# A four-layer graph network on one core: tables between merges and node stages as 4 KB lines by partition

## The reference

```
L0: h = normalised(h W^T + b) * gate;   agg = softmax-weighted sum of h[src] over dst; then a bounded size
L1: agg = sum of weight * (h W_nbr)[src] over dst;  + h W_own + bias
L2: z = leaky((h W_s^T)[src] + (h W_t^T)[dst]);  softmax over src;  sum of h[src] * share over dst, times W_fc^T
L3: messages of 64 features from h[src], four heads, softmax over dst;  sum over dst
```

## Time and profile before

| what | time |
|---|---|
| median of 3 runs | 8230.51 us (8223.3 to 8243.03) |
| profiled execution | 8246.78 us, its span 8245.1 us |
| busy, of the span | PE 71%, PEld 44%, DVE 63%, ACT 38%, POOL 59% |
| DMA | 1450.33 MB, mean 176 GB/s |
| queues (packets, MB, share of 16 engines) | q1: 236788, 752.87, 26.6%; q10: 413792, 410.91, 15.6%; q0: 150656, 285.54, 12.3% |

### The profile page before, as it was taken

How to read it: one execution, slowest core, us unless ns; L and a number is a source line. 1 busy time by engine, 2 the same in 40 slices (tenths; PEclk the granted TensorE clock), 3 DMA queues, 4 the chain that set the end, 5 groups by cost and what they waited for, 6 DMA issues and landing times. The chain is left out here.

```text
span 8245.1 us, 149719 instructions
## 1 busy us (share of the span) xinstructions
PE 5872.9 (71%) x21822; PEld 3639.1 (44%) x21823; DVE 5193.8 (63%) x17420; ACT 3106.2 (38%) x9803; POOL 4876.8 (59%) x6036
## 2 busy tenths in 40 slices
PE   4997999046769998676999877677666769600476
PEld 3771344025544444454444344444324558500365
DVE  5999888034569996455666555555773549633764
ACT  2990355004555553355444311111112557400156
POOL 1557777757622223764777677777567743477442
PEclk8995899568999999898999988888897989855799
DMA  2661000027966665697888755555105987522267
GB/s 90 211 209 19 1 1 1 1 84 238 306 227 246 245 246 192 203 301 258 314 313 311 278 187 188 188 192 184 41 12 177 294 276 226 163 54 55 62 214 228
DMA packets 801333, 1450.33 MB, mean 176 GB/s; under 512 B 136831, under 2 KB 543383, under 8 KB 801236
## 3 DMA queue, kind: packets, MB, share of 16 engines
q1 hardware_dynamic: 236788, 752.87, 26.6%
q10 hardware_dynamic: 413792, 410.91, 15.6%
q0 software_dynamic: 150656, 285.54, 12.3%
HBM read 803.24 MB, written 645.70 MB: 176 GB/s over the span
## 5 line engine op out<-in xcount | busy, mean ns | idle before, releaser
L1176 PE MATMUL merge_banks<-merge_rows,merge_mask 128*128 x6264 | 1648.1, 420 | 686.8 <-SPq L1145 406.1
L1176 PEld LDWEIGHTS merge_banks<-merge_rows,merge_mask 128*128 128x128 f32 x6264 | 1264.8, 209 | 1070.1 <-issue 885.9
L1158 DVE TENSOR_SCALAR merge_mask<-ramp,dst_at,soft_at_step 128x128 f32<-128x128 f32 x2349 | 843.2, 366 | 987.7 <-PE merge_banks L1176 862.0
L1270 POOL DMA_INDIRECT merge_rows<-h,merge_take_i x1176 | 1127.5, 959 | 565.5 <-issue 291.9
L1812 PE MATMUL node_p_out<-w,node_h_t 128*128 128x259 f32 (+2 forms) x4704 | 1439.2, 429 | 26.9 <-ACT node_h_t L1851 25.6
L1208 ACT COPY merge_total<-merge_banks 128x256 f32<-128x256 f32 x1568 | 577.4, 369 | 1164.3 <-PE merge_banks L1176 1053.8
L1725 POOL TENSOR_TENSOR node_inv_std<-node_var,node_minus_half 128x4 f32<-128x4 f32 x392 | 445.8, 1137 | 872.5 <-DVE node_var L1662 537.5
L1812 PEld LDWEIGHTS node_p_out<-w,node_h_t 128*128 128x128 f32 x4704 | 746.7, 191 | 286.7 <-issue 217.4
L1790 PE MATMUL node_p_turn<-ident,node_xn 128*128 128x128 f32 x3136 | 619.7, 280 | 187.4 <-DVE node_xn L1619 100.2
L1812 PE MATMUL node_p_out<-w,node_kept_t 128*128 128x512 f32 x1568 | 741.4, 596 | 0.0
L1790 PEld LDWEIGHTS node_p_turn<-ident,node_xn 128*128 128x128 f32 x3136 | 407.7, 142 | 725.0 <-issue 449.3
(11 more groups left out here) (485 smaller groups left out, 10602.6 us busy)
## 6 DMA issues: line engine op xcount, KB each, us to landing
merge_held<-own ACTq DMA_DIRECT2D x196, 512.0 KB
x<-merge_total ACTq DMA_DIRECT2D x196, 512.0 KB
node_x<-x SPq DMA_DIRECT2D x196, 512.0 KB, 6.2
node_x<-in_x SPq DMA_DIRECT2D x194, 512.0 KB
h<-node_rows_h SPq DMA_DIRECT2D x98, 512.0 KB
merge_held<-h ACTq DMA_DIRECT2D x98, 512.0 KB
mix<-merge_total ACTq DMA_DIRECT2D x98, 512.0 KB
node_mixed<-mix SPq DMA_DIRECT2D x98, 512.0 KB, 4.2
```

The lines of the kernel that those rows point to most:

```text
L1158: ins = nc.vector.tensor_scalar(mask[j][:], k.ramp[:, 0:P], columns(k.dst_at, s), columns(weight, s), ALU.is_equal, ALU.mult)
L1176: nc.tensor.matmul(banks[:, bass.ds(nc.s_assert_within(at[2 * j + 1], 0, (BANKS - 1) * 512, skip_runtime_bounds_check_because=small), D)], ...
L1270: nc.gpsimd.indirect_dma_start(rows[:, (j + n) * D:(j + n + 1) * D], None, table, bass.IndirectOffsetOnAxis(take_i[:, j + n:j + n + 1], 0) ...
```

## The change

The tables that go from a merge to a node stage or from a node stage to a merge's base (mix0, own1, x2, own2, x3) get the turned shape: one line of 4 KB for each partition of a group, tiles as runs of 128 nodes. Node stages 1 to 3 therefore also take their nodes as tiles of 128 neighbours. So in_x of stage 1 is loaded by `tile_rows` (with one more DMA for the last 80 rows, and 16 more to wait for), and the tables that are gathered by node (h1, from_src, to_dst, h2, h3) are stored by `tile_rows`: pieces of 1 KB, of 544 B for h3. Node stage 0, the table h0, merge 0's base and the output of merge 3 stay as they are. Not a byte more is moved, and no compute instruction is added or removed.

```
 merge, hold(q):
-                act.dma_start(held[q.h][:], tile_rows(base, q.H * ROWS)).then_inc(held_got[q.h], 16)
+                if base.shape[1] == G * D:
+                    act.dma_start(held[q.h][:].rearrange("p g f -> p (g f)"), turned_group(base, q.H)).then_inc(held_got[q.h], 16)
+                else:
+                    act.dma_start(held[q.h][:], tile_rows(base, q.H * ROWS)).then_inc(held_got[q.h], 16)
 merge, flush(q):
-                if whole:
+                if out.shape[1] == G * D:
+                    act.dma_start(turned_group(out, q.H), total[q.h][:].rearrange("p g f -> p (g f)")).then_inc(put[q.h], 16)
+                elif whole:
                     act.dma_start(tile_rows(out, q.H * ROWS, whole), total[q.h][:, 0:whole, :]).then_inc(put[q.h], 16)
 node_pass, load(q):
-                sp.dma_start(mixed[q.h][:], group_rows(mixed_in, q.H * ROWS)).then_inc(mixed_got[q.h], 16)
+                sp.dma_start(mixed[q.h][:].rearrange("p g f -> p (g f)"), turned_group(mixed_in, q.H)).then_inc(mixed_got[q.h], 16)
 node_pass, load_x(q):
-                sp.dma_start(x[q.h][0:rows // G], group_rows(x_in, base, rows)).then_inc(x_got[q.h], 16)
+                if layer >= 2:
+                    sp.dma_start(x[q.h][:].rearrange("p g f -> p (g f)"), turned_group(x_in, q.H)).then_inc(x_got[q.h], 16)
+                elif layer == 1:
+                    whole, part = rows // P, rows % P
+                    sp.dma_start(x[q.h][:, 0:whole, :], tile_rows(x_in, base, whole)).then_inc(x_got[q.h], 16)
+                    if part:
+                        begin = base + whole * P
+                        sp.dma_start(x[q.h][0:part, whole, :], x_in[begin:begin + part, :]).then_inc(x_got[q.h], 16)
+                else:
+                    sp.dma_start(x[q.h][0:rows // G], group_rows(x_in, base, rows)).then_inc(x_got[q.h], 16)
 node_pass, store_tables(q):
-                    sp.dma_start(group_rows(table, q.H * ROWS), part).then_inc(t_put[q.h], 16)
+                    if table.shape[1] == G * D:
+                        sp.dma_start(turned_group(table, q.H), part.rearrange("p g f -> p (g f)")).then_inc(t_put[q.h], 16)
+                    elif layer == 0:
+                        sp.dma_start(group_rows(table, q.H * ROWS), part).then_inc(t_put[q.h], 16)
+                    else:
+                        sp.dma_start(tile_rows(table, q.H * ROWS), part).then_inc(t_put[q.h], 16)
 node_pass, average_tile(q, g):
-                    dve.wait_ge(x_got[q.h], 16 * (q.i + 1))
+                    dve.wait_ge(x_got[q.h], 16 * (q.i + 1) + (16 if layer == 1 and q.final and x_in.shape[0] % P else 0))
 score_sources, store(q):
-                sp.dma_start(group_rows(h_out, q.H * ROWS), h[q.h][:]).then_inc(h_put[q.h], 16)
+                sp.dma_start(tile_rows(h_out, q.H * ROWS), h[q.h][:]).then_inc(h_put[q.h], 16)
 gnn_kernel:
-        mix0, own1, x2, own2, x3 = (dram(n, (k.NP, D)) for n in ("mix0", "own1", "x2", "own2", "x3"))
+        mix0, own1, x2, own2, x3 = (dram(n, (k.NT // G * P, G * D)) for n in ("mix0", "own1", "x2", "own2", "x3"))
```

## The result

| | before | after |
|---|---|---|
| median | 8236.23 us (8 runs, 8223.3 to 8252.1) | 8259.24 us (8 runs, 8247.3 to 8267.84) |
| ratio to before | | 1.0026, 95% interval 1.0015 to 1.0038: +21 us (12 to 31) |
| profiled execution, its span | 8246.78, 8245.1 us | 8265.3, 8263.6 us |

The forecast was +12 us, inside no change; the result is just outside. The page after answers the table ahead of the prediction: the same bytes, q10's packets down to less than half, q1's nearly doubled.

A forecast was written before the change was run, and what follows sets the result against it. Bounds: ScalarE in the merges' last groups, store waits in node stages 1 and 2, TensorE and VectorE in stage 3, POOL in the scores. Terms -12 - 15 + 15 + 22 + 2 = +12 us gave 8242 us, range 8215 to 8272.

The forecast's parts named there:

- Node stage 2, +22: Node stage 2: from_src and to_dst in 1 KB pieces lengthen the stage; 22 us taken, bounds 0 and 53.
- the turned store is the last of four in order: 0.54 us later: Node stage 2: two stores in pieces delay the turned store by 2 x 0.22 + 2 x 0.05 us; VectorE's chain follows.
- Rival 1: Node stages 1 and 2: bursts become the bound, each group pays the whole delay, +102 us; 8306 us, chance 0.20.
- Node stage 1, +15: Node stage 1: in_x and h1 in 1 KB pieces lengthen the stage; 15 us taken, bounds 0 and 49.
- own lands 0.18 + 0.22 us later: Node stage 1: in_x's load and h1's store in pieces delay own; with dearer issues 0.5 us, 0.25 us a group.
- Merges, -12 for the issues: Merges: 395 ScalarE issues by 4 KB lines, each 30 ns cheaper; 12 us less, bounds 0 to 20.
- Merges, -15 for the gap of each fourth group: Merges 0 to 2: ScalarE's long gap in every fourth group shrinks, 6 + 6 + 3 = 15 us less; bounds 0 and 37.
- the work of the queue falls by 14.5%, so half of the excess goes: Merges 1 and 2: less HWDGE work removes half of the 0.19 us a group over merge 3; a quarter in merge 0.
- Node stage 3, +2, and source scores, 0: Node stage 3: h3 in 544 B pieces, 2 us taken. Source scores: h2 in 1 KB pieces, 0 taken, bounds 0 and 22.
- rival 4: Node stage 3: h3's small pieces set the pace, +28 us; 8268 us, chance 0.08.
- Rival 2: Merges: DMA is the bound, 30 us less in merges 1 and 2 each, 15 in merge 0; 8182 us, chance 0.17.
- rival 3: Whole kernel: piece size does nothing, only issues get cheaper, -12 us; 8218 us, chance 0.17.

The follow-up runs named there:

- experiment 2: Before, with node stage 2 storing from_src and to_dst in 1 KB pieces: 8281.99 us, 1.0039 of before.
- experiment 1: After, with node stage 2 storing from_src and to_dst as 4 KB runs again: 8241.69 us, 0.9989 of before.
- experiment 3: After, with node stage 2's own2 store first in the burst, on its own semaphore, for which alone VectorE waits: 8248.99 us, 0.9997 of before.
- experiment 4: Before, with node stage 2's own2 store first in the burst, on its own semaphore: 8251.9 us, 1.0004 of before.
- experiment 10: After, with in_x (node stage 1) loaded and to_dst (node stage 2) stored as 4 KB runs again; another chip: 1.0015 of before.
- experiment 11: After, with h1 stored as 4 KB runs in node stage 1, in_x still loaded in pieces; another chip: 1.0028 of before.
- experiment 5: After, with everything node stages load and store by node as 4 KB runs again, leaving the merges' part: 8228.22 us, 0.9983 of before.
- experiment 6: After, with node stage 1's load of mixed and store of own cut into 1 KB pieces too: 1.0027 of before.
- experiment 7: After, with own2 first on its own semaphore in node stage 2, and h1 and own on separate semaphores in node stage 1: 8217.7 us, 0.9968 of before.
- experiment 8: After, with the merges' loads and stores of partition-line tables cut into 1024 pieces of 512 B: 8302.17 us, 1.0074 of before.
- experiment 9: Before, with own2 first on its own semaphore (node stage 2), h1 and own on separate semaphores (node stage 1); another chip: 0.9982 of before.
- experiment 12: After, with node stage 2's load of x2 in 1 KB pieces too; another chip: 1.0032 of before.

## Why the prediction was right or wrong

It forecast +12 us, and +21 (12 to 31) was measured. The sign is right and the sum near, but that is luck in part: two of its terms were off by 15 us each, in opposite directions.

**Node stage 2, +22: right.** Measured +27.5 in the profiles and +32 by experiment 2. The step "the turned store is the last of four in order: 0.54 us later" measured 0.70: its landing after its own issue went from 5.75 to 6.18 us, +0.43 (forecast 0.44 for two stores in pieces), and it is issued 0.27 later (forecast 0.10; SP's issue of a store in pieces is 383 ns against 332, and later issues of the burst stretched too). After differs from before in more than the two stores; the pieces alone (experiment 2 against before, experiment 1 against after) delay the landing after its own issue by 0.33 and 0.26 us and the issue by 0.37, 0.71 and 0.64 together. So the sum of the step was near, its split was not. "Idle stands once in two groups" gives 0.35 us a group by that delay, the chain over three groups 0.23; measured is 27.9/97 = 0.29. Rival 1's full 0.70 a group, 69 us, did not come. Experiments 3 and 4 show that it is this loop: cut, the pieces cost under 1 us.

**Node stage 1, +15: wrong, nothing.** The failed step is "own lands 0.18 + 0.22 us later". I added the engines' time of two transfers running alone to the landing of a third. The engines' work did grow by just that (q1's share 68.9% to 73.7% of 600 us is 0.41 us a group), but they were idle for a quarter of the stage, and own landed 0.45 us sooner after its issue, 0.16 sooner counted from the burst's first issue. Experiments 10 and 11 take the two apart: h1's store in pieces does delay own, by 0.1 us and not 0.22, and in_x's load in pieces, put at 0.18 later, lets it land 0.3 us sooner. That a longer loop would cost time isn't refuted: no run here lengthened it by more than 0.12 us, and cutting it gave 18 us.

**Merges, -12 for the issues: right.** ScalarE's issues by lines take 362 to 374 ns instead of 402 (forecast 372), and the gap that holds them is shorter (0.94 us against 0.97 in the earlier trace rows; the second row is of the long gap):

```profile
2202.51 0.37 ACT L1211 COPY merge_total<-merge_banks 128x256 f32<-128x256 f32 x1 [0.94 <-PE merge_banks L1176]
2208.78 0.37 ACT L1211 COPY merge_total<-merge_banks 128x256 f32<-128x256 f32 x1 [3.36 <-PE merge_banks L1176]
```

**Merges, -15 for the gap of each fourth group: wrong.** The last 65 groups gained 3.6, 4.8 and 4.8 us in merges 0 to 2, and 0.2 in merge 3, 13 in all. The issues give 1.8, 5.0, 5.0 and 1.6 of that. In merges 0 to 2 the 16 long groups got shorter by 0.12, 0.09 and 0.00 us in the mean, the others by 0.04, 0.07 and 0.10: beyond the others nothing (16 x 0.01 = 0.2 us), not 15. (The 3.36 us above against 3.73 in the earlier trace rows is one pair out of a spread.) The step that failed is "the work of the queue falls by 14.5%, so half of the excess goes". Its first half came in part: q10's time per MB fell by 6% in merge 0 (forecast 7), from 69.2% of 45.02 MB to

```profile
q10 hardware_dynamic: 29525, 46.10, 66.4%
```

and by 8 and 9% in merges 1 and 2 (200 us of each; forecast 14.5), where the DMA share went from 0.91 to 0.87 (named as the sign: 0.84). The second half put the gap down to DMA without a row for it, and there is one: the sequencer's read of the counts. In merge 0 before, in merge 3 before, and in merge 0 after:

```profile
L1121 ACTq TENSOR_LOAD <-merge_flush_at x16: 1613/2018/2602, 2062.0 to 2337.7; - x16
```

```profile
L1121 ACTq TENSOR_LOAD <-merge_flush_at x16: 558/1766/1965, 7972.4 to 8236.0; - x16
```

```profile
L1121 ACTq TENSOR_LOAD <-merge_flush_at x16: 1439/1792/2895, 2061.9 to 2333.2; - x16
```

Without the short one in the last groups, the mean read took 2.12, 2.15 and 2.04 us in merges 0 to 2 before, and 1.99, 2.12 and 2.09 after: most of the long gap, and not clearly shorter with lines. In merge 3 it took 1.78 before. So 15 x 0.34 = 5 us of the 12 by which merge 0's last 65 groups exceed merge 3's are this read; why it is longer where rows are gathered isn't shown.

**Node stage 3, +2, and source scores, 0: right.** h3's 544 B pieces raised the stage's DMA share from 0.74 to 0.80, not to the pace-setting level of rival 4; its time stayed. What I did not see is +3 us ahead of merge 3's first store: from node stage 3's last load it took 643 to 645 us in the six kernels of the first chips whose merge 3 loads x3 as 4 KB lines (after, experiments 1, 3, 5, 6 and 7), 641 to 642 in before and experiments 2, 4 and 8. Its cause is open.

The two misses, 15 us each with opposite signs, cancelled. Rival 2 (merges are DMA's, 87 us less) and rival 3 (piece size does nothing) are refuted by experiments 5 and 2. The Trainium skill's line-rate rule (DMA: Bandwidth & Descriptors, "Specifications") counts every transfer of 512 B or more as at line rate. Of the time this case agrees with it where the loop was cut: 1 KB pieces cost under 1 us. Of the engines' work it disagrees: at that same time the DMA share was 0.97 against 0.89, and for the same 410.91 MB q10's share of the span was 14.5% in after, 15.6% before and 17.0% with the merges in 512 B pieces (experiment 8). For the landing of a store that something waits for it disagrees too: two stores in 1 KB pieces ahead of it made it land some 0.3 us later after its own issue (0.33 and 0.26, experiments 2 and 1).

## What to carry to other kernels

Price a transfer's change where somebody waits: first find which landing releases the loop, what is issued ahead of it in the same burst, and how far the loop stands above the next bound; here one stage stood 5 us above it and lost 28, another had 18 us to give back and lost none. The engines' time for a transfer running alone is not the delay of one that lands behind it: here two stores in pieces cost the store behind them 0.26 to 0.33 us (0.44 forecast), one cost 0.1 (0.22 forecast), and a load in pieces let it land 0.3 sooner (0.18 later forecast). When a wait counts several stores of one burst, give the store whose buffer is needed a semaphore of its own and put it first: two such edits took 48 us off after and 0.18% off before (experiments 7 and 9), and with them the node stages no longer cared about piece size. And when an engine has a gap, look at its sequencer's instructions in the gap before pricing it by what runs beside it.

## What the runs showed of the hardware

- In the median a DMA's issue on ScalarE or SP costs by form, not by the number of pieces: 402 ns on ScalarE for stores in 512 and in 1024 pieces, 362 to 374 for 128 unbroken lines; 383 against 332 for from_src on SP. A difference of 10 ns says nothing: merge 3's store, the same in both kernels, took 402 ns before and 413 after. Later issues of a burst are longer (from_src to turned in after: 383, 458, 898, 1201 ns), and of 98 x 2 loads in 1024 pieces 19 took over 0.62 us, up to 2.07 (experiment 8).
- A load in 1 KB pieces ahead of stores in the same queue let the last of them land 0.3 us sooner, counted from the burst's first issue, than a load in 4 KB runs; the same behind them did not (experiments 10, 11 and 12).
- The sequencer's read of a loop's counts on ScalarE (TENSOR_LOAD) took 2.0 to 2.2 us in the mean in the last 65 groups of merges 0 to 2, before and after, more than the two DMA issues beside it.
- Chips differ by stage: the kernel before took 9570 us on one and 8243 us on another. By experiment 9's profile, node stages 1 to 3 and merge 3 are alike there, it takes 700 us more ahead of merge 0's first store, some 400 more from the source scores to the end of merge 2, and 87 and 97 more in the stretches of merges 0 and 1. The merges' gain from longer lines wasn't seen there.
